# A two-layer decoder on one core: the attention division moved onto head rows, and more of the matmuls cut into four column tiles of 32

## What is computed

```python
# layer 0
x = layernorm(x + banded_attention_block(x))         # 8 heads of 32, keys within 64 tokens
x = layernorm(x + causal_cross_attention(x, ctx))    # 16 heads of 16, 1601 keys
x = layernorm(x + mixture_with_lora(x))
# layer 1
x = layernorm(x + self_attention(x))                 # 16 heads of 16, 2048 keys
x = layernorm(x + cross_attention(x, ctx, mask))     # 16 heads of 16, 1601 keys
x = layernorm(x + mixture_of_8_experts(x))
# every attention: softmax(q k^T * scale) v, heads joined, then @ Wo + bo
```

## Time and profile before

| | us |
|---|---|
| median of 3 runs | 3220.12 (3219.56 to 3221.94) |
| profiled execution | 3225.91 |
| its span | 3224.2 |
| PE busy in the span | 2839.3 (88%) |
| DVE busy | 2066.7 (64%) |
| ACT busy | 1569.2 (49%) |

### The profile page before, as it was taken

One profiled execution on the slowest core, in us unless ns is written; L12 is line 12 of the kernel. 1 busy time (PEld: TensorE's weight loads), 2 busy tenths in 40 slices (PEclk: granted clock), 3 DMA queues, 4 the chain that ended last, 5 costly groups with the idle time before them and its releaser, 6 DMA issues. The chain is left out here.

```text
span 3224.2 us, 68849 instructions
## 1 busy us (share of the span) xinstructions
PE 2839.3 (88%) x27534; PEld 1379.9 (43%) x27535; DVE 2066.7 (64%) x4240; ACT 1569.2 (49%) x2122; POOL 223.7 (7%) x295
## 2 busy tenths in 40 slices
PE   6677987999996997799999999999999999379992
PEld 3455552333334454134434344443433333246661
DVE  4335137888765225778989898988998995312224
ACT  2223222655663222256777776776676768123331
POOL 2001201000001001210000000000000000210003
PEclk9788997999998998699999999999999999589996
DMA  5422023011000002412122112111121110711112
GB/s 158 106 46 79 14 80 99 1 37 37 1 1 14 24 0 86 121 42 60 33 61 51 36 51 55 49 34 50 43 58 44 44 44 2 253 43 33 33 33 87
DMA packets 112813, 172.51 MB, mean 54 GB/s; under 512 B 17882, under 2 KB 88427, under 8 KB 112147
## 3 DMA queue, kind: packets, MB, share of 16 engines
q1 hardware_dynamic: 109460, 160.11, 17.6%
q0 software_dynamic: 3072, 8.39, 0.8%
HBM read 127.63 MB, written 40.51 MB: 52 GB/s over the span
## 5 line engine op out<-in xcount | busy, mean ns | idle before, releaser
L1292 DVE TENSOR_REDUCE d_part_max<-d_ps_m 128x1 f32<-128x512 f32 (+1 forms) x1964 | 1128.1, 631 | 92.0 <-PE d_ps_m L1279 55.9
L1601 ACT ACTIVATE d_prob<-d_ps_s 128x1024 f32<-128x1024 f32 x928 | 898.8, 1021 | 346.9 <-PE d_ps_s L1470 340.2
L1279 PE MATMUL d_ps_m<-k_st,q_st 97*32 97x512 bf16 (+1 forms) x5296 | 481.2, 362 | 20.0 <-DVE d_part_max L1292 16.5
L1470 PE MATMUL d_ps_s<-q_st,k_st 98*32 98x512 bf16 x5104 | 441.4, 382 | 9.8 <-ACT d_prob L1601 8.4
L684 DVE TENSOR_REDUCE x_part_max<-x_att_ps_m 128x1 f32<-128x512 f32 (+2 forms) x578 | 311.2, 587 | 72.4 <-PE x_att_ps_m L663 32.3
L924 ACT ACTIVATE x_att_prob<-x_att_ps_s 128x1024 f32<-128x1024 f32 (+3 forms) x296 | 259.3, 919 | 161.7 <-PE x_att_ps_s L806 94.4
L1488 PE MATMUL d_ps_o<-d_prob,a_values 128*32 128x512 f32 x2048 | 267.5, 596 | 0.0
L1279 PEld LDWEIGHTS d_ps_m<-k_st,q_st 97*32 97x32 bf16 x5296 | 143.2, 96 | 273.0 <-DVE d_part_max L1292 128.5
L1279 PE MATMUL d_ps_m<-q_st 97*32 97x512 bf16 (+1 forms) x2560 | 232.5, 362 | 2.2 <-DVE d_part_max L1292 0.4
L1470 PEld LDWEIGHTS d_ps_s<-q_st,k_st 98*32 98x32 bf16 x5104 | 138.3, 97 | 194.9 <-issue 82.9
L1488 PE MATMUL d_ps_o<-d_prob,x_values 128*32 128x512 f32 x1664 | 215.5, 593 | 0.4 <-ACT d_prob L1601 0.4
(11 more groups left out here) (326 smaller groups left out, 3252.2 us busy)
## 6 DMA issues: line engine op xcount, KB each, us to landing
k_st<-parts_k SPq DMA_DIRECT2D x90, 256.0 KB, 5.7
k_st<-parts_k SPq DMA_DIRECT2D x90, 208.0 KB, 4.8
l_w<-in_l_w SPq DMA_DIRECT2D x16, 1024.0 KB, 11.7
q_st<-parts_q SPq DMA_DIRECT2D x48, 256.0 KB, 4.9
q_st<-parts_q SPq DMA_DIRECT2D x192, 64.0 KB
q_st<-parts_k SPq DMA_DIRECT2D x30, 256.0 KB
q_st<-parts_k SPq DMA_DIRECT2D x30, 208.0 KB
parts_q<-a_proj_parts SPq DMA_DIRECT2D x16, 384.0 KB, 2.5
```

Source lines behind the costliest of these rows:

```text
L1279: mm = pe.matmul(bank[q:q + COLUMNS, 0:w], self.query(s, h, ROW_MASK + 1, a * P + q, COLUMNS), self.key(s, h, ROW_MASK + 1, k, w), start=T ...
L1292: dve.tensor_reduce(self.part[:, h * QT + a, i:i + 1], bank[:, 0:w], AX.X, ALU.max).then_inc(s_read, 1)
L1470: mm = pe.matmul(ps_s[u][k:k + COLUMNS, hh, :], maxima.key(s, h, ROW_MAX + 1, kt * P + k, COLUMNS), maxima.query(s, h, ROW_MAX + 1, 0, QC) ...
L1601: act.activation(prob[:, p % 2, 2 * u:2 * u + 2, :], ps_s[u][:, :, :], ACT.Exp, scale=scale).then_inc(s_prob, 1)
```

## The change

Three things change.

1. **Layer 0's attentions**: max products, scores and the products that add the masks are issued as four matmuls of 32 columns each. Their division stays as it was.
2. **The stream's division**: `turn_out`, `turn_tokens` and `copy_tokens` go. SP copies each head's 16 output rows from `o_raw` to their place in feature-major `o_fm`, and its denominator row 16 times into `den`: eight transfers a step (`gather`). When half of the features of a chunk are there, DVE takes the reciprocal of `den` in place (128 rows of 512) and multiplies (16 times in all). `normalise` stands three pairs after the end of every second step (`GATHERED_AT`); for the last one it stands at once. The close of a chunk moves by no more than one pair.
3. **The stream's output, projection and value products** are issued as four column tiles of 32.

```diff
 # Maxima.product, layer 0 (scores and masks of attend are cut in the same way)
-            mm = pe.matmul(out, q_st[0:rows, slot, j, t * P:(t + 1) * P], k_st[0:rows, slot, j, k:k + w],
-                           start=(half == 0), stop=(half == at.halves - 1 and not masked))
+            for q in range(0, P, COLUMNS):
+                start = t * P + q
+                mm = pe.matmul(out[q:q + COLUMNS, :], q_st[0:rows, slot, j, start:start + COLUMNS],
+                               k_st[0:rows, slot, j, k:k + w], start=(half == 0),
+                               stop=(half == at.halves - 1 and not masked), skip_group_check=True)
...
 # Plan
-    TURN_AT = 2
+    GATHERED_AT = 3
...
-            start = self.out_at[NG * k + NG - 1]
+            start = self.gathered_at[NG * k + NG - 1]
             for a in range(QT):
-                self.tasks[start + 1 + a].append(("turn", k, a))
-                self.tasks[start + 2 + a].append(("prod", k, a))
+                self.tasks[start + 1 + a].append(("prod", k, a))
...
 # decoder_attention, SP, at the first pair after step s, ahead of load
+            def gather(s):
+
+                k, g = s // NG, s % NG
+                sp.wait_ge(s_ocopy, s + 1)
+                if k >= 1:
+                    sp.wait_ge(s_norm, halves_done(s) - DT + 1)
+                if k >= 2:
+                    sp.wait_ge(s_prod, QT * (k - 1))
+                for j in range(GH):
+                    first = (g % (NG // DT) * GH + j) * SH
+                    rows, m = slice(first, first + SH), g // (NG // DT)
+                    sp.dma_start(den[rows, m, :], o_raw[32 * j + SH:32 * j + SH + 1, :]
+                                 .rearrange("p (o n) -> p o n", o=1).to_broadcast((1, SH, QC))).then_inc(s_gather, 16)
+                    sp.dma_start(o_fm[rows, k % 2, m, :], o_raw[32 * j:32 * j + SH, :]).then_inc(s_gather, 16)
...
 # PE: out_product (units and values are cut in the same way)
                 for m in range(DT):
-                    mm = pe.matmul(plan.bank(step)[:, 0:D], o_fm[:, n % 2, m, :],
-                                   wo_sb[:, plan.chunks[k][0], m, :], start=(m == 0), stop=(m == DT - 1))
+                    for q in range(0, P, COLUMNS):
+                        start = a * P + q
+                        mm = pe.matmul(plan.bank(step)[q:q + COLUMNS, 0:D],
+                                       o_fm[:, k % 2, m, start:start + COLUMNS],
+                                       wo_sb[:, plan.chunks[k][0], m, :], start=(m == 0), stop=(m == DT - 1),
+                                       skip_group_check=True)
...
 # DVE: normalise, now for every second step, 128 rows of 512
+                half = halves_done(s)
+                k, m = half // DT, half % DT
+                dve.wait_ge(s_gather, 16 * 2 * GH * (s + 1))
+                dve.reciprocal(den[:, m, :], den[:, m, :]).then_inc(s_inv_den, 1)
+                dve.wait_ge(s_inv_den, half + 1)
+                dve.tensor_tensor(o_fm[:, k % 2, m, :], o_fm[:, k % 2, m, :], den[:, m, :],
+                                  ALU.mult).then_inc(s_norm, 1)
```

More of the change, by code:

```diff
@@ L39 @@
 SH = 16
+COLUMNS = 32
 NSH = D // SH
@@ L1119, in __init__ @@
         self.chunks = [(si, c) for si in range(len(segments)) for c in range(NQ)]
-        self.out_at = [self.first[s + 1] + (self.TURN_AT if s + 1 < len(self.steps) else 1)
-                       for s in range(len(self.steps))]
+        self.gathered_at = [self.first[s + 1] + (self.GATHERED_AT if s + 1 < len(self.steps) else 0)
+                            for s in range(len(self.steps))]
         self.place_entries()
@@ L1307 @@
 V_STEP = SH + 1
-COLUMNS = 32
 def value_block(values, i, h):
@@ L1424, in _ @@
                         maxima.send(sp, s, s_mred, x - plan.ahead + 1)
+                for s in range(len(plan.steps)):
+                    if plan.first[s + 1] == p:
+                        gather(s)
                 for s in range(2, len(plan.steps)):
@@ L1490, in times_v @@
                 mm.then_inc(s_pv, 1)
[L1492 to L1499, removed]
-                mm.then_inc(s_turn, 1)
-            def turn_tokens(step):
-                k, a = step[1:]
-                pe.wait_ge(s_norm, NG * (k + 1))
-                bank_free(step)
-                for m in range(DT):
-                    mm = pe.transpose(plan.bank(step)[:, m * P:(m + 1) * P], o_tok[:, k % 2, a, m * P:(m + 1) * P],
-                                      cst["ident"][:, :])
-                mm.then_inc(s_oturn, 1)
             def out_product(step):
@@ L1546, in unit_product @@
                 for d in range(DT):
-                    mm = pe.matmul(plan.bank(step)[:, 0:n], w_sb[:, 0 if side == "q" else 1, d, m * P:(m + 1) * P],
-                                   src[:, d, k:k + n], start=(d == 0), stop=(d == DT - 1))
+                    for q in range(0, P, COLUMNS):
+                        start = m * P + q
+                        mm = pe.matmul(plan.bank(step)[q:q + COLUMNS, 0:n],
+                                       w_sb[:, 0 if side == "q" else 1, d, start:start + COLUMNS],
+                                       src[:, d, k:k + n], start=(d == 0), stop=(d == DT - 1), skip_group_check=True)
                 mm.then_inc(s_mm, 1)
@@ L1571, in _ @@
                     maxima_products(plan.places[p][3])
[L1572 to L1574 removed]
                 for task in plan.tasks[p]:
[L1576 to L1578 removed]
+                    if task[0] == "prod":
                         out_product(task)
```

109 lines of the change are left out of this document (43 added, 66 removed).

## The result

Before 3219.84 us (3217.27 to 3222.75), after 3238.96 us (3234.97 to 3247.86), six runs each: ratio 1.0062, 95% interval 1.0047 to 1.0077, so 19.1 us slower. The forecast was 3252, +32. The profiled executions have spans of 3224.2 and 3239.4 us, 15.2 apart.

The account below looks back on a forecast made before the run. PE was taken to bound the kernel, with DVE close behind. Terms -29 - 4 + 3 - 47 + 99 + 10 = +32 us gave 3252 us, 1.0% slower; range 3205 to 3285, likeliest case 3238 to 3268.

Parts of the forecast that it names:

- x0: Attention stage x0: all-tiled products save PE 0.23 us a pair over 148 pairs, after deductions 29 us saved.
- Banded attention and projections: Layer 0: tiling saves 4 us in the banded attention; mixed product kinds in the projections ahead lose 3 us.
- the issue-bound rival: Banded attention: narrow tiles limited by instruction issue, up to 80 us more, 3332 us at most; chance 0.06.
- The stream's gain: Stream: PE saves 47 us from dropped transposes, shorter output products and fewer changes of product kind.
- The output products: Stream: 32 output products, tiled and without the next token tile's transpose, fall to 0.86 us each, saving 18.5 us.
- The units and value tiles: Stream: 16 units and 13 value tiles each lose two changes of product kind, saving 8 us.
- The reciprocal: Stream's division on DVE: a 512-column reciprocal takes 4.4 us, from the steepest slope of 8.3 ns a column.
- that rival: Stream's division: reciprocal takes 3.4 us at the flattest slope, 16 us less, total 3236 us; chance 0.10.
- What PE loses by a normalise: Stream: each normalise costs PE 4.2 us of waiting plus 2.4 at half clock, 99 us over fifteen.
- The rival in which the clock holds: Stream: PE's waits behind normalises do not bring 1.2 GHz, so 36 us go, total 3216; chance 0.18.
- its rival: Stream's gather lands 2 to 3 us later than counted, adding 30 to 45 us, 3282 to 3297; chance 0.10.
- The end: End of the stream, last copy to last statistics: 20.7 us instead of 10.8, 10 us more.

Follow-up runs that it names:

- alone: Kernel before with only layer 0's attentions in column tiles, old division and stream kept: ratio 0.9929 of the kernel before.
- experiments 5 and 6: Changed kernel with each normalise in four pieces of 128 columns, six pairs apart (0.9967 of before) or in four successive pairs (1.0006).
- experiment 9: Changed kernel with one reciprocal per denominator (128x32), inverses spread through HBM, multiply on DVE, chunk close five pairs later: ratio 0.9869 of before.
- experiment 7: Changed kernel with each normalise in two pieces of 256 columns, six pairs apart: ratio 1.0025 of the kernel before.
- experiment 5: Changed kernel with each normalise in four pieces of 128 columns, six pairs apart: ratio 0.9967 of the kernel before.

## Why the prediction was right or wrong

The sign, the mechanism and its place were right; the terms erred in both directions, and it is partly luck that the total came as close as it did. Of the signs that were named, four came: idle time of PE before a max product behind each normalise (3.0 to 3.2 us in place of 4), half clock with it, the shorter distance in x0, and no transposes of the old division. One did not: the reciprocal is 3.34 us, not 4.4.

- **x0: -29, measured -24.0** (-22.8 alone). The 0.23 us a pair is there: the median distance from value product to value product fell from 2.92 to 2.68. 35 us of it over the pairs; the part that PE doesn't get, 11 us, is larger than the 5 that I took off. PE's idle time in x0 rose from 10.2 to 14.2 us, which explains 4 of the 6.
- **Banded attention and projections: -4 and +3**, measured -5.2 and +3.6. The narrow tiled products cost nothing extra, so the issue-bound rival is out. The Trainium skill (TensorEngine Tiling, Restrictions) says that column tiling turns fast weight load off; at these sizes neither of layer 0's attentions became longer by it.
- **The stream's gain: -47, measured -32.9** (the kernel without reciprocals). Per self-attention chunk 4.6 us, per cross-attention chunk 3.7, where 5.9 were counted. (This kernel still has the multiply, 0.69 us of hold sixteen times.) The distances from one value product to the next, pair by pair, show which terms were too large. A pair with `turn_out` fell from 3.37 to 2.69 us, 0.68 as counted. The output products, counted at 18.5 us with their transposes, gave some 10: the product became as short as I said (0.86), but its pair fell from 3.99 us only to 3.55 in self-attention, and in cross-attention from 4.05 to 4.58 only to 3.75 to 4.58. The units and value tiles, counted at 8, gave some 3. What failed is that I took every microsecond off PE as a microsecond off the pair and gave back only 2 us for DVE. DVE sets part of the pace already: in self-attention such a pair now takes exactly what its four reductions, the add and the statistics take on DVE, 3.55 us (timelines of DVE, then PE, no reciprocals):

```profile
1737.29 0.42 DVE L1717 TENSOR_TENSOR x_tok<-x_tok,d_ps_m 128x256 f32<-128x256 f32 x1
...
1738.30 2.45 DVE L1302 TENSOR_REDUCE d_part_max<-d_ps_m 128x1 f32<-128x512 f32 x4
1740.84 0.42 DVE L1717 TENSOR_TENSOR x_tok<-x_tok,d_ps_m 128x256 f32<-128x256 f32 x1
...
1736.16 1.07 PE L1528 MATMUL d_ps_m<-d_wo,d_o_fm 128*32 128x256 f32 x16
...
1739.71 1.07 PE L1528 MATMUL d_ps_m<-d_wo,d_o_fm 128*32 128x256 f32 x16
```

- **The reciprocal: 4.4 us, measured 3.34.** (3344 - 249) / 496 = 6.2 ns a column, the flattest slope of the earlier trace rows, which I had listed as a rival and given 0.10; that rival's own time, 3236, is the nearest to the 3239 measured.
- **What PE loses by a normalise: 6.6 us x 15 = 99, measured 5.35 x 15 = 80.2.** The rule for the wait held: 4.2 us for a hold of 5.05, so 3.2 for 4.03, and the waits are 2.99 to 3.18 (3.72 at the first) plus what a drawn product hides. The clock's part was 2.4 us each as counted (35.7 / 15). The rival in which the clock holds is out for waits of 3 us. For waits of half a microsecond to one it is right but for one stretch in experiments 5 and 6; between 1.3 and 2.1 us the clock sometimes falls and sometimes not.
- **The gather** was hidden, by about 1 us; its rival is out. A late transfer did cost, but in my own kernel, experiment 9.
- **The end: +10, measured +7.0** from score to router, 7.5 from copy to statistics. Of the 2.4 us between the 20.7 counted and the 18.3 there, 1.0 is the shorter reciprocal and 1.4 the four output products: 5.4 us for 6.8, since the clock was back after two of them (0.67 over the four).
- **Not foreseen: -12.3 behind the stream.** 6.8 of it are in the experts, 324.7 to 317.9 us, and all nine other kernels with the moved division have 317.1 to 318.1, the three with the old one 323.7 to 324.7. A tile there takes 7.98 us in place of 8.14 (medians of 38): the first output product starts 0.05 us closer behind the two transposes before it, and the second 0.15. The code there is the same, so the cause stays open. The rest, about 5 us in the last stretch, is scatter: with the same code that stretch is 51.5 to 58.1 us long.

The gains of x0 and the stream were taken 19 us too high, the loss and the end 22 too high, and 12 us came unforeseen: the total was 17 us off in the spans and 13 in the medians because the first two cancel. That they do is luck.

## What to carry to other kernels

Before a small operation on an engine that isn't the bottleneck is made wide to save work elsewhere, look at how long it holds that engine in one go: here 4.0 us on DVE cost PE 3.1 us of waiting and 2.4 more at half clock. Cutting the hold into pieces takes away the clock's part and little else; the rest goes only with the work. And a value that is copied sixteen times to make shapes fit should be computed before it is copied: 32 columns instead of 512 turned 19 us lost into 42 to 50 us gained.

## What the runs showed of the hardware

- At each of PE's fifteen waits of 3.0 to 3.7 us the granted clock fell to 0.50: for 6.8 us where it fell before the wait's end (eight times), for 3.4 where it fell up to 1.4 us after it. Waits of 6.4 to 7.1 us brought 6.8 or 10.2 us of it.
- Shorter waits brought it only sometimes: three of the eight of 2.1 us in experiment 7, and, over all the kernels here, ten of 36 waits of 1.4 to 1.5 us for ACT's exponentials, 3.4 us each. None of the some sixty waits of 0.3 to 1.3 us in experiment 5 did. What decides in between no run shows.
- Reciprocals on DVE: 249 ns for 16 columns, 343 for 32, 942 for 128, 1742 for 256, 3344 for 512: about 6.2 ns a column all the way.
- A power of -1 on POOL takes 82 us for 512 columns, 25 times DVE's reciprocal; a multiply 1.27 us against 0.69.
